# Linear attention on one Trainium2 core: features a tile further ahead, housekeeping and gathers moved, a projection in row tiles

## The reference

```python
q, k = relu(x @ Wq.T) + 1e-6, relu(x @ Wk.T) + 1e-6     # per head
kv_cum = cumsum(einsum('bhsd,bhsm->bhsdm', k, v), axis=2)
out = einsum('bhsd,bhsdm->bhsm', q, kv_cum)
z = 1.0 / (einsum('bhsd,bhsd->bhs', q, cumsum(k, axis=2)) + 1e-6)
x = x + (out * z[..., None]) @ Wo.T
```

## Time and profile before

| what | value |
|---|---|
| median of 3 runs | 2453.93 us (2449.8 to 2454.33) |
| the profiled execution | 2452.73 us, span 2451.0 us |
| mean granted TensorE clock in it | 0.888 of full |
| `project`, about | 0 to 140 us of the span |
| `linear`, about | 1629 to 2119 us |
| busy in the span | PE 78%, DVE 67%, ACT 44%, POOL 69% |

### The profile page before, as it was taken

The page is one execution under the profiler, slowest core; times in us unless marked ns, Lnnn a source line. Parts: engine busy times, 40 slices in busy tenths (PEclk is TensorE's granted clock), DMA queues, the critical chain, the costliest instruction groups (busy, mean ns, idle before and its releaser), DMA issues. The chain is left out here.

```text
span 2451.0 us, 48548 instructions
## 1 busy us (share of the span) xinstructions
PE 1918.8 (78%) x12428; PEld 1048.8 (43%) x12557; DVE 1653.8 (67%) x4337; ACT 1078.2 (44%) x1728; POOL 1687.2 (69%) x1184
## 2 busy tenths in 40 slices
PE   7869999999999999999956629956776777310797
PEld 3423333333333333333345528843444444200697
DVE  5757777777777777777647764426888888660354
ACT  6824555555555554555523315522444444212243
POOL 3537888888888888888836763348888876217365
PEclk9969999999999999999965659987999999555799
DMA  6863221222122122212123324440000000122232
GB/s 197 280 206 111 69 67 56 66 69 63 58 69 67 57 65 69 63 57 69 40 65 99 113 81 127 126 157 24 20 17 20 20 19 9 39 59 104 82 103 66
DMA packets 159713, 192.86 MB, mean 79 GB/s; under 512 B 28793, under 2 KB 113792, under 8 KB 159648
## 3 DMA queue, kind: packets, MB, share of 16 engines
q1 hardware_dynamic: 144816, 161.83, 21.8%
q0 software_dynamic: 13824, 29.43, 3.7%
q10 hardware_dynamic: 1008, 0.92, 0.1%
HBM read 110.48 MB, written 82.10 MB: 79 GB/s over the span
## 5 line engine op out<-in xcount | busy, mean ns | idle before, releaser
L612 DVE TENSOR_REDUCE halfmax<-p_m 128x1 f32<-128x512 f32 x1024 | 665.3, 681 | 247.6 <-PE p_m L500 228.1
L481 POOL TENSOR_TENSOR sum_p<-sum_p,probs 128x1024 f32<-128x1024 f32 x320 | 753.5, 2355 | 40.0 <-ACT probs L607 22.0
L607 ACT ACTIVATE probs<-p_s 128x1024 f32<-128x1024 f32 x512 | 522.1, 1024 | 483.7 <-PE p_s L525 401.6
L500 PE MATMUL p_m<-ka,qa 128*128 128x512 bf16 x992 | 384.7, 388 | 40.6 <-DMA vh<-v 19.2
L525 PE MATMUL p_s<-qb,kb 66*128 66x512 bf16 x1024 | 390.9, 382 | 15.3 <-ACT probs L607 9.6
L524 PE MATMUL p_s<-qa,ka 128*128 128x512 bf16 x927 | 353.6, 381 | 3.3 <-ACT probs L607 0.9
L532 PE MATMUL p_o<-probs,vh 128*32 128x256 f32 x4096 | 274.0, 385 | 0.0
L481 POOL TENSOR_TENSOR sum_p<-probs 128x1024 f32<-128x1024 f32 x64 | 150.0, 2344 | 138.7 <-ACT probs L607 138.7
L1495 PE MATMUL ln_p_cum<-ln_kv,c_tri 128*128 128x512 f32 (+1 forms) x384 | 162.0, 563 | 67.5 <-POOL ln_kv L1439 67.4
L500 PEld LDWEIGHTS p_m<-ka,qa 128*128 128x128 bf16 x1024 | 99.6, 97 | 243.7 <-DVE halfmax L612 149.9
L1149 ACT ACTIVATE e_h<-e_p_h,e_w 128x256 f32<-128x256 f32 x316 | 126.3, 474 | 173.7 <-PE e_p_h L1128 173.4
...
...
## 6 DMA issues: line engine op xcount, KB each, us to landing
qa<-q SPq DMA_DIRECT2D x128, 128.0 KB, 2.7
ka<-k SPq DMA_DIRECT2D x128, 128.0 KB, 2.8
...
```

Source lines behind the costliest of these rows:

```text
L481: nc.gpsimd.tensor_tensor(sum_p[s % 2][:, :], (sum_p[s % 2] if n else probs[0])[:, :], probs[k][:, :], ALU.add).then_inc(sum_p_d, 1)
L500: nc.tensor.matmul(max_bank(s, n)[:, :], qa[s][:, (n // 2) * P:(n // 2 + 1) * P], ka[s][:, (n % 2) * HALF:(n % 2 + 1) * HALF], start=True, ...
L607: nc.scalar.activation(probs[k][:, :], p_s[k % 2][:, :], ACT.Exp, scale=SCALE).then_inc(probs_d, 1)
L612: nc.vector.reduce_max(halfmax[s % 2][:, n % 2, n // 2:n // 2 + 1], max_bank(s, n)[:, :], AX.X).then_inc(max_read, 1)
```

## The change

In `project` the weights that contract over 64 rows (`wku`, `wvu`) are held twice, on partitions 0 to 63 and 64 to 127, and so is the latent `lat`: `wd` has its 64 columns twice. The two matmuls for k, and the four for v in the order 0, 2, 1, 3, alternate between the two halves of the PE array by `tile_position`. Seven weight loads stand where four stood.

In `linear`:
- Layout. Each head's denominator becomes a ninth column of its numerators (`M1` = 9), in `v1`, `kv`, `p_cum`, `raw`, `state` and `p_prev`. The product is one instruction of 1152 instead of 128 and twice 512, the sum over d one reduction of 1152 instead of two, the state mask one of 144 instead of 128 and 16. The total numerator is written to PSUM (`p_prev[:, 144:288]`) instead of SBUF, and the division reads it there.
- DVE. `attend_tile` is split into `product` and `quotient`, and `features` of tile n+2 stands between them, where features of n+1 stood ahead of tile n. For t = 2 it stands behind step 4 of `choose` instead. The steps of `choose`, which alternated with the "a" steps at t = 0, stand at t = 2; `shift_logits` goes from t = 3 to the next t = 0; `add_output` stands behind `scales`.
- POOL. `outer` is for tile n+2 instead of n+1 and stands behind the gathers and the gate instead of ahead of them; the gathers are 2, 3, 3 and 0 a tile instead of 3, 3, 2 and 0.
- PE and ACT. Their orders follow. On PE the group transposes go behind `sums`; at t = 2 `project_tile` goes behind `turn_first` and `earlier`. On ACT `keep_values` is for n+2.

```diff
@@ -39,7 +39,9 @@
 HALF = 512
 SCALE = float(DH0) ** -0.5
 H1, DH1 = 16, 8
-KV1 = H1 * DH1 * DH1
+M1 = DH1 + 1
+KV1 = H1 * M1 * DH1
+ST1 = H1 * M1
...
-                sp.dma_start(dst[:, :], src).then_inc(w_in, 16)
+            sp.dma_start(wq[:, :], w["WqT"]).then_inc(w_in, 16)
+            for i in range(2):
+                half = slice(i * LR, (i + 1) * LR)
+                for dst, src in ((wd[:, half], w["WdT"]), (wku[half, :], w["WkuT"]), (wvu[half, :], w["WvuT"])):
+                    sp.dma_start(dst, src).then_inc(w_in, 16)
...
                     for cc in range(2):
-                        mm = nc.tensor.matmul(p_qk[:, 2 + cc, :], wku[:, cc * P:(cc + 1) * P], lat[:, :], start=True, stop=True)
+                        half = slice(cc * LR, (cc + 1) * LR)
+                        mm = nc.tensor.matmul(p_qk[:, 2 + cc, :], wku[half, cc * P:(cc + 1) * P], lat[half, :], start=True, stop=True,
+                                              tile_position=(cc * LR, 0))
...
-                        mm = nc.tensor.matmul(p_v[:, t, :], lat[:, t * P:(t + 1) * P], wvu[:, :], start=True, stop=True)
+                    for t in (0, 2, 1, 3):
+                        half = slice(t // 2 * LR, (t // 2 + 1) * LR)
+                        mm = nc.tensor.matmul(p_v[:, t, :], lat[half, t * P:(t + 1) * P], wvu[half, :], start=True, stop=True,
+                                              tile_position=(t // 2 * LR, 0))
                     mm.then_inc(pv_d, 1)
...
                 i = g[1]
-                for n in ((0, 1, 2), (3, 4, 5), (6, 7), ())[t]:
+                for n in ((0, 1), (2, 3, 4), (5, 6, 7), ())[t]:
...
-                    nxt = next_tile(g, t)
+                    second = next_tile(g, t, 2)
                     if exists(g):
                         keep_state(g, t)
-                    if exists(nxt[0]):
-                        outer(*nxt)
                     if exists(after(g, 2)):
                         if t == 0:
                             take_slots(after(g, 2))
                         gather(after(g, 2), t)
                         if t == 3:
                             gate(after(g, 2))
-
-            pool.wait_ge(S["mask"], 6)
+                    if exists(second[0]):
+                        outer(*second)
...
+                        turn_q(*nxt)
+                        sums(*nxt)
                     if t == 2 and exists(after(g)):
                         turn_first(after(g))
                     if t == 3 and exists(before):
                         turn_second(before)
                     if exists(nxt[0]):
-                        add_state(*nxt)
-                    if exists(second[0]):
+                        earlier(*nxt)
+                    if t == 2 and exists(second[0]):
                         project_tile(*second)
                     if t == 0 and exists(before):
                         output_rows(before)
                     if t == 3 and exists(before):
                         router(before)
-                    if exists(nxt[0]):
-                        turn_q(*nxt)
-                        sums(*nxt)
-                        earlier(*nxt)
 
...
-            def attend_tile(g, t):
+            def product(g, t):
                 n, tb, s = tile_number(g, t), g[1] * G + t, t % 2
                 q = qk[s][:, 0:D].rearrange("p (h d) -> p h d", h=H1)
                 dve.wait_ge(S["cum"], n + 1)
                 from_first(dve, "o", n)
-                nc.vector.tensor_tensor(prod[:, KV1:KV1 + D], p_cum[:, 2, 0:D], qk[s][:, 0:D], ALU.mult).then_inc(S["prod"], 1)
-                for a in range(2):
-                    hs = slice(a * H1 // 2, (a + 1) * H1 // 2)
-                    last = nc.vector.tensor_tensor(prod[:, a * 512:(a + 1) * 512].rearrange("p (h m d) -> p h m d", d=DH1, m=DH1),
-                                                   p_cum[:, a, :].rearrange("p (h m d) -> p h m d", d=DH1, m=DH1),
-                                                   q[:, hs, :].unsqueeze(2).broadcast_to([P, H1 // 2, DH1, DH1]), ALU.mult)
-                last.then_inc(S["prod"], 1)
-                dve.wait_ge(S["prod"], 2 * n + 1)
-                nc.vector.tensor_reduce(den[:, :], prod[:, KV1:KV1 + D].rearrange("p (h d) -> p h d", h=H1), AX.X, ALU.add).then_inc(S["den"], 1)
-                dve.wait_ge(S["prod"], 2 * n + 2)
-                nc.vector.tensor_reduce(num[:, :].rearrange("p (h m) -> p h m", h=H1),
-                                        prod[:, 0:KV1].rearrange("p (h m d) -> p h m d", h=H1, d=DH1), AX.X, ALU.add).then_inc(S["num"], 1)
-                dve.wait_ge(S["den"], 3 * n + 1)
+                nc.vector.tensor_tensor(prod[:, :].rearrange("p (h m d) -> p h m d", h=H1, m=M1),
+                                        p_cum[:, 0:KV1].rearrange("p (h m d) -> p h m d", h=H1, m=M1),
+                                        q.unsqueeze(2).broadcast_to([P, H1, M1, DH1]), ALU.mult).then_inc(S["prod"], 1)
+                dve.wait_ge(S["prod"], n + 1)
+                parts = prod[:, :].rearrange("p (c d) -> p c d", d=DH1)
+                if tb > 0:
+                    nc.vector.tensor_reduce(num[:, :], parts, AX.X, ALU.add).then_inc(S["num"], 1)
+                else:
+                    nc.vector.tensor_reduce(p_prev[:, ST1:2 * ST1], parts, AX.X, ALU.add).then_inc(S["num"], 2)
+
+            def quotient(g, t):
+                n, tb = tile_number(g, t), g[1] * G + t
+                whole = p_prev[:, ST1:2 * ST1]
                 if tb > 0:
                     dve.wait_ge(S["prev"], prevs(g[0], tb))
-                    nc.vector.scalar_tensor_tensor(out=den[:, :], in0=den[:, :], scalar=FEAT_EPS,
-                                                   in1=p_prev[:, D:D + H1], op0=ALU.add, op1=ALU.add).then_inc(S["den"], 1)
-                    dve.wait_ge(S["num"], n + 1)
-                    nc.vector.tensor_tensor(num[:, :], num[:, :], p_prev[:, 0:D], ALU.add)
-                else:
-                    nc.vector.tensor_scalar(den[:, :], den[:, :], FEAT_EPS, None, ALU.add).then_inc(S["den"], 1)
-                dve.wait_ge(S["den"], 3 * n + 2)
+                    dve.wait_ge(S["num"], 2 * n + 1)
+                    nc.vector.tensor_tensor(whole, num[:, :], p_prev[:, 0:ST1], ALU.add).then_inc(S["num"], 1)
+                two = whole.rearrange("p (h m) -> p h m", h=H1)
+                dve.wait_ge(S["num"], 2 * n + 2)
+                nc.vector.tensor_scalar(den[:, :], two[:, :, DH1], FEAT_EPS, None, ALU.add).then_inc(S["den"], 1)
+                dve.wait_ge(S["den"], 2 * n + 1)
                 nc.vector.reciprocal(den[:, :], den[:, :]).then_inc(S["den"], 1)
-                dve.wait_ge(S["den"], 3 * n + 3)
+                dve.wait_ge(S["den"], 2 * n + 2)
                 if t == 0:
                     from_first(dve, "poT", number(g))
-                nc.vector.tensor_tensor(o[:, t, :].rearrange("p (h m) -> p h m", h=H1), num[:, :].rearrange("p (h m) -> p h m", h=H1),
+                nc.vector.tensor_tensor(o[:, t, :].rearrange("p (h m) -> p h m", h=H1), two[:, :, 0:DH1],
                                         den[:, :].unsqueeze(2).broadcast_to([P, H1, DH1]), ALU.mult).then_inc(S["o"], 1)
...
-                    if exists(next_tile(g, t)[0]):
-                        features(*next_tile(g, t))
+                    second = next_tile(g, t, 2)
                     if exists(g):
-                        attend_tile(g, t)
+                        product(g, t)
+                    if t != 2 and exists(second[0]):
+                        features(*second)
+                    if exists(g):
+                        quotient(g, t)
                     if t == 0:
-
-                        for first, step in ((clip, 0), (add_moe, 1), (None, 2), (statistics, 3), (moments, 4), (variances, 5), (None, 6)):
-                            if first and exists(coming):
-                                first(coming, *(("a",) if first in (statistics, moments, variances) else ()))
-                            if exists(choosing):
-                                choose(choosing, step)
+                        if exists(choosing):
+                            shift_logits(choosing)
+                        if exists(coming):
+                            clip(coming)
+                            add_moe(coming)
+                            statistics(coming, "a")
+                            moments(coming, "a")
+                            variances(coming, "a")
                     if t == 1:
-                        if exists(before):
-                            add_output(before)
                         if exists(coming):
                             scales(coming, "a")
                         if exists(before):
+                            add_output(before)
                             statistics(before, "c")
                             moments(before, "c")
                             variances(before, "c")
-                    if t == 2 and exists(before):
```

(14 more changed lines are left out.)

90 lines of the change are left out of this document (48 added, 42 removed).

## The result

The changed kernel takes 2528.26 us (median of 4 runs, 2525.25 to 2537.05) against 2454.13 us of the kernel before: ratio 1.031, 95% interval 1.0293 to 1.0326. It is 74 us slower; 2438 was forecast. The profiled execution has a span of 2528.4 us against 2451.0, and a mean granted clock of 0.866 against 0.888.

A forecast was written before the change was run, and what follows sets the result against it. POOL was taken as nearly full, with a chain through PE, ACT and DVE at t = 2. Loop -11.2, last two groups -2.9, projection -1 gave -15.1 us: about 2438, forecast case 2430 to 2445, whole range 2415 to 2451.

The forecast's parts named there:

- 26.6 us a group: Loop of `linear`: POOL's own 25.3 us plus 1.3 idle at t = 2, against 27.4 before.
- slower: Rival in `linear`: DVE instructions stall beside POOL's long ones, three a group, 29.7 us a group, 2481 us; chance 0.13.
- POOL's own work: Loop of `linear`: 25.85 us a group falls by 0.56 to 25.3 through the single state mask.
- DVE's own work: Loop of `linear`: 23.2 us a group plus 0.56 for the tile and 1.22 for de-interleaved housekeeping, 25.0.
- The product of 1152: DVE's one product instruction in `linear`, at 1.03 ns a column: 1.34 us.
- The quotient stalls no more: DVE's `ln_o` in `linear`, reading PSUM, stops stalling beside POOL: 1.5 us a group no longer lost.
- The projection: `project` with matmuls alternating between two halves of the PE array: -1 us, ends nothing and -5.
- 0.14 to the sums: PE at t = 2 in `linear`: sums start 0.14 us after the end of the outer product before.
- the 5.4 us at t = 2: `linear`, outer product to next: sums, transposes, projection, features, copy of v; POOL has 4.1 us of work, idles 1.3.
- The last two groups: End of `linear`, without gathers, DVE as the bound: 47.1 us instead of 50.0, so -2.9.
- the 1.6 from which it was said to cost anything: Rival of stalled DVE instructions in `linear`: costs only above 26.6 - 25.0 = 1.6 us a group.
- Slow sums: Rival: after PE's longer wait one set of sums takes 3.90 instead of 2.20 us, +1.7 a group, 2440 to 2450; chance 0.10.

The follow-up runs named there:

- pe_order: Changed kernel with the next group's transposes and first projection ahead of the sums again at t = 2 on PE; period 30.22 us, ratio 1.0142.
- late_projection: layout_only with the next group's transposes and first projection behind the sums at t = 2, ACT's turned copy behind the queries; period 30.27 us, ratio 1.0172.
- act_order: Changed kernel with ACT's copies of the sums to `raw` ahead of the normalisations at t = 2 and 3; period 31.41 us, ratio 1.021.
- layout_only: Changed kernel's layout and projection row tiles, with every engine's order as in the kernel before; period 27.46 us, ratio 0.9977.
- eps_only: Changed kernel with eps of both norms added inside ACT's square root instead of by DVE, order unchanged; period 30.58 us, ratio 1.0178.

## Why the prediction was wrong

**The sign and the size.** Forecast were 26.6 us a group and 2438 us (2437.6 and 1.2 give 2438.8); measured 33.05 and 2528. The rival "slower" got a chance of 0.13 and a price of 2481, 27 us of a loss of 74.

**What held.** POOL's own work: 25.3 forecast, 25.2 measured. DVE's own work, 25.0 forecast: in the group above DVE waits 0.58, 0.58, 0.81 and 2.27 us for PE and loses 1.46 + 1.76 us in two stalls; 32.66 less these 7.46 is 25.2. The product of 1152: 1.34 forecast, 1.36. The quotient stalls no more. The projection: within measurement of nothing.

**The step that failed.** "From the end of the outer product before: 0.14 to the sums", the first term of the 5.4 us at t = 2. It took over from the earlier trace rows that sums follow their outer product at once. In the changed kernel they start 3.8 us after it, because `p_cum` exists once and DVE is not done with the product of t = 2. Measured, the way from the end of one outer product to the start of the next is 1990.13 - 1978.57 = 11.56 us where 5.4 stood: 3.79 to the sums instead of 0.14; 3.97 instead of 2.20 until the transposes start behind them; 2.71 instead of 2.24 to the end of the projection; 1.09 to the outer product. And behind it I wrote "26.6 a group, against DVE's own 25.0", as if the larger of two sums were the period. The chain and DVE are not two candidates: the chain goes through DVE. The features of the next group's first tile wait on DVE for the projection, and the product of t = 3 waits behind the features; the projection waits behind the sums of t = 3, and these for the product of t = 2. So DVE's own work, its stalls and its waits add up: 25.2 + 3.2 + 4.2 us in that group. pe_order takes the projection out of this chain and gains 2.8 us (33.05 to 30.22). late_projection puts it behind the sums in a kernel without the other orders and loses 2.8 (27.46 to 30.27); DVE waits 4.78 us for the projection in its group, though there the sums still follow their outer product at once. So the wait behind the sums is shown on both sides, and the 3.79 instead of 0.14 by the rows of the changed kernel.

**The last two groups.** They were forecast at 47.1 us, 2.9 less than before. From the product of group 14 to the last quotient they take 53.5 instead of 50.0. DVE waits 5.8 us in them for PE, which the forecast had at nothing; without these waits 47.7 are left. It is the same step: DVE's work was taken for the whole time.

**What I left out.** ACT's queue. I costed no wait for `raw`, though `keep_sums` stands behind the normalisation and PE's `add_state` waits for it: 1.6 us a group by act_order.

**The rival "slower" named the mechanism and the wrong victims.** It had the clip, the add into `X` and the steps of `choose` beside POOL's instructions. Clip (median 426 ns) and add (693) are as before; it is `rstd_a` and `shift_a` that stall, 3.2 us in the group above and 3.0 a group over the loop. With every order of before, in layout_only, it was the clip. The price of it, 2.5 us by eps_only and 3.0 beside the two orders, is above the 1.6 from which it was said to cost anything. The Trainium skill ("SBUF — State Buffer", section "Who interferes with whom") says that a DVE instruction with two SBUF inputs contends with a GpSimd instruction that reads SBUF, and so may a `tensor_scalar` from SBUF to SBUF. `shift_a` is of the first kind and `rstd_a` of the second: by that rule, the trace agrees (medians of 162 ns before and 1924 now, 151 and 1506). The page says of no instruction here how often it will meet the other; that came from the order.

**Slow sums** were a rival too, with +1.7 once a group. In the group above two sets take 3.55 and 4.18 us, the other two 2.10 and 2.21: the granted clock fell to 0.50 behind the waits. Of the 11.56 us above, sums and turns that ran longer than the rows of before are 2.2 (1.77 and 0.47). Over the loop the four sets of a group take 12.2 us where they took 10.0; in pe_order it is 10.2, and from layout_only to late_projection it goes from 10.4 to 11.8. So 1.9 of the 2.8 us of pe_order and 1.5 of the 2.8 of late_projection could be sums at the lower clock. They aren't the whole of the loss: eps_only gains 2.5 us a group with 27 of 56 sets over 3.3 us, 4 more than the changed kernel. No run takes the clock apart from the waits that go with it, so its share of the 5.5 us stays open.

Undoing the PE order (2.8), the ACT order (1.6) and the eps instruction (2.5) alone gives 6.9 in all, and the three together give 7.0. That accounts for the loss of 5.5 and leaves 1.45 a group of gain, which no run takes apart: features of n+2, gathers in front, the layout and the own work of the eps instructions (some 0.3) are in it; 0.8 to 0.9 was forecast without the latter.
